# A graph network on one core: zero products left out of three gather loops, four waits put before GpSimd's gathers

## What is computed

```python
x = _layernorm(x + _L0_gnn_ref(x, L0_gnn_weights, src, edge_type_8, dst))  # per relation: mean of x[dst] over (src, type), times W[type]
x = _layernorm(x + _L1_gnn_ref(x, edge_index, ...))   # GCN: sum of dinv[src]*dinv[dst]*h[src] over dst, batch norm
x = _layernorm(x + _L2_gnn_ref(x, edge_index, ...))   # GATv2: 4 heads, scores of leaky_relu(xl[src]+xr[dst]), softmax over dst, feed forward
x = _layernorm(x + _L3_gnn_ref(x, edge_index, ...))   # two transformer convolutions: q[dst].k[src], softmax over dst, sum of attn*v[src]
```

## Time and profile before

| | us |
|---|---|
| median of 3 runs | 3878.28 (3877.59 to 3880.7) |
| the profiled execution | 3893.77 |
| its span, first to last instruction | 3892.1 |

### The profile page before, as it was taken

How to read it: one execution, slowest core, us unless ns; L and a number is a source line. 1 busy time by engine, 2 the same in 40 slices (tenths; PEclk the granted TensorE clock), 3 DMA queues, 4 the chain that set the end, 5 groups by cost and what they waited for, 6 DMA issues and landing times. The chain is left out here.

```text
span 3892.1 us, 57650 instructions
## 1 busy us (share of the span) xinstructions
PE 2947.8 (76%) x14303; PEld 2002.8 (51%) x14345; DVE 2492.3 (64%) x8135; ACT 1048.7 (27%) x2557; POOL 2423.7 (62%) x2427
## 2 busy tenths in 40 slices
PE   6987997746666567999977999766677776676773
PEld 3455895534444433444435777643465564364663
DVE  8886553251111377999988888873567775384876
ACT  3730664110000043333315666620011120010211
POOL 2747777647777347777754666117777734777770
PEclk8975557568888788999988999888798898888986
DMA  2222222322222147888851222026787755687872
GB/s 70 68 60 52 62 62 58 48 61 53 53 53 53 29 90 197 239 236 236 241 138 57 68 70 70 22 78 181 196 243 223 226 167 139 182 245 194 252 238 65
DMA packets 397387, 493.91 MB, mean 127 GB/s; under 512 B 64035, under 2 KB 293992, under 8 KB 397138
## 3 DMA queue, kind: packets, MB, share of 16 engines
q0 software_dynamic: 92160, 244.83, 24.3%
q1 hardware_dynamic: 304978, 245.98, 21.8%
HBM read 376.23 MB, written 114.36 MB: 126 GB/s over the span
## 5 line engine op out<-in xcount | busy, mean ns | idle before, releaser
L1918 POOL DMA_INDIRECT got<-kv_table,pair_src x832 | 839.3, 1009 | 495.4 <-issue 249.3
L686 POOL DMA_INDIRECT y_got<-y_table,y_idx x416 | 399.7, 961 | 166.2 <-issue 126.4
L1164 POOL DMA_INDIRECT got<-t_table,tile_src x392 | 378.3, 965 | 175.4 <-issue 118.8
L2167 PE MATMUL psum<-acc 125*128 x1664 | 285.1, 324 | 219.0 <-DVE h L1984 195.1
L1313 PE MATMUL sums<-msg,hot 128*125 128x260 f32 x1664 | 394.0, 390 | 31.3 <-POOL msg L1255 28.6
L2167 PEld LDWEIGHTS psum<-acc 125*128 125x128 f32 x1664 | 243.7, 224 | 297.1 <-issue 295.8
L2179 PE MATMUL psum<-h,acc 128*128 128x128 f32 x1664 | 324.0, 329 | 68.1 <-ACT hot_b L2142 37.3
L1313 PEld LDWEIGHTS sums<-msg,hot 128*125 128x125 f32 x1664 | 305.9, 189 | 119.1 <-issue 72.3
L1984 DVE TENSOR_TENSOR h<-psum,got 128x512 f32<-128x512 f32 x208 | 143.4, 690 | 348.1 <-DMA got<-kv_table,pair_src 315.1
L1255 POOL TENSOR_TENSOR msg<-rows,msg 128x512 f32<-128x512 f32 x208 | 246.3, 1204 | 188.1 <-DVE msg L1281 148.7
L628 PE MATMUL psum<-zeros 128*128 128x512 bf16 (+1 forms) x946 | 340.6, 490 | 3.5 <-issue 2.4
(11 more groups left out here) (506 smaller groups left out, 5705.3 us busy)
## 6 DMA issues: line engine op xcount, KB each, us to landing
v_rows<-got SPq DMA_DIRECT2D x208, 256.0 KB, 3.4
small<-v_rows SPq DMA_DIRECT2D x208, 256.0 KB, 4.8
dst_row<-dst_rows SPq DMA_DIRECT2D x312, 128.0 KB, 4.8
rows<-x_rows SPq DMA_DIRECT2D x104, 256.0 KB
x_rows<-small SPq DMA_DIRECT2D x104, 128.0 KB, 3.6
x_rows<-got_w SPq DMA_DIRECT2D x104, 128.0 KB, 4.5
got<-kv_table,pair_src POOLq DMA_INDIRECT x832, 3.8
y_table<-y_stage SPq DMA_DIRECT2D x25, 448.0 KB
```

The source lines that it names most:

```text
L686: pool.indirect_dma_start(out=got[:, slot, j, :], out_offset=None, in_=y_table[:, :], in_offset=bass.IndirectOffsetOnAxis(ap=m.y_idx[:, co ...
L1164: pool.indirect_dma_start(out=got[:, col % ring, :], out_offset=None, in_=table[:, :], in_offset=bass.IndirectOffsetOnAxis(ap=m.tile_src[: ...
L1918: pool.indirect_dma_start(out=got[:, slot, j, :], out_offset=None, in_=kv_table[:, :], in_offset=bass.IndirectOffsetOnAxis(ap=m.pair_src[: ...
L2167: last = t.matmul(work[:, j * P:(j + 1) * P], hot_t[:, g % 2, j // 2, j % 2, :], m.acc[:, bass.ds(ws[j], 1), 0:D].rearrange("q o d -> q (o ...
```

## The change

It takes three of the four calls of the helper out: 4 zero products behind each of 38 groups of the relation loop, 6 behind each of 92 groups of the GCN loop, 6 in each of 60 groups of each transformer. And it puts one more wait before GpSimd's DMAs in four loops: in the scatters of the sort for TensorE's `placed`, in the first ring of the relation's gathers for `counted`, in the GAT's gathers for `z_done` (all four sums of group g - 4 are made before the gathers of group g), in the transformers' for `q_done` (the queries of group g - 7 are spread before the gathers of group g).

```diff
@@ sort_edges, gpsimd
             for t in range(BY_DMA):
+                if 6 * t // 5 > 8:
+                    pool.wait_ge(placed, 6 * t // 5 - 8)
                 pool.indirect_dma_start(out=code_table[:, :], ...
@@ relation_layer, gpsimd
                 if g >= SL:
                     pool.wait_ge(used, g - SL + 1)
+                elif g > 2:
+                    pool.wait_ge(counted, min(4 * g - 8, groups))
@@ relation_layer, tensor
                 last.then_inc(used, 1)
-                if g >= 2 * SL:
-                    keep_busy(t, psum[0:Q, 6 * 512:7 * 512], zeros, Q, 4)
@@ gcn_sums, tensor
                 last.then_inc(used, 1)
-                if g < tile_groups - ROOM:
-                    keep_busy(t, sums[0:Q, 6 * 512:7 * 512], zeros, Q, 6)
@@ gat_scores, gpsimd
                 if g >= slots:
                     pool.wait_ge(turned, g - slots + 1)
                     pool.wait_ge(scored, (g - slots) // 2 + 1)
+                    pool.wait_ge(z_done, 4 * (g - 3))
                     pool.wait_ge(aside[slot], 32 * (g // slots))
@@ conv_layer, gpsimd
                 slot = g % 8
+                if g >= 7:
+                    pool.wait_ge(q_done, g - 6)
                 if g >= 8:
@@ conv_layer, tensor
                     for s in sums_due(c, k):
                         add(c - 1, s)
-                    if not len(sums_due(c, k)):
-                        keep_busy(t, psum[:, 0:512], zeros, P, 6)
```

## The result

The change makes the kernel slower by half a per cent: 3900.22 us median of 5 (3893.84 to 3908.23), beside 3879.77 for the kernel before (3877.59 to 3880.7). The ratio is 1.0056, interval 1.0043 to 1.0069, which is 17 to 27 us. The forecast was 3885, range 3877 to 3893. By the prediction's own line of 0.2% this is "slower", its second likeliest direction (0.42), and the time lies outside the range.

The account below looks back on a forecast made before the run. GpSimd's issue of gathers, 1.25 us each, was taken to bound the loops. Relation tail -1.7, transformer tails +0.75 and GAT wait +8.1 made +7.15 us on the median 3878.3: 3885, range 3877 to 3893.

Parts of the forecast that it names:

- The zero products in the loops: Relation, GCN and transformer loops: removing the products lowers TensorE's clock, but idle time hides it; cost 0.
- (c): Rival, loops: the lower TensorE clock costs time where cover is thin, up to 232 us; chance 0.02.
- The tails: Ends of loops: relation gains 1.7 us, GCN 0, transformers lose 0.75; -3 to +3 kept for the clock's phase.
- The waits that should not bind: Sort, relation's first ring, transformers: the added waits pass without a gap; cost 0, bounds 0 to 1 us.
- The wait that does bind: GAT gathers: waiting for the sums of group g - 4 stops GpSimd; +8.1 us, bounds 3.5 to 13.5.
- The release: GAT: a gather starts 0.74 us after the end of TensorE's sum, a figure taken from VectorE's releases.
- the prediction's replay: GAT, 98 groups recomputed by four rules from one trace's landings: 19 stops sum to 9.6 us, net +8.1.
- (b): Rival, GAT: the wait sets the loop's pitch, by later landings or slow TensorE groups; +13 to +18, 3891 to 3896; chance 0.18.
- The base: Whole kernel: the sum is added to the median 3878.3; the profiled execution's 15.5 us above it don't matter.
- (a): Rival, GAT: the wait passes after all, by faster release or earlier landings; +3 or less, 3877 to 3880; chance 0.22.
- (e): Rival, all four loops: the added waits never hold; counted as the same case as (a), without its own chance.
- (d): Rival, transformers: gathers themselves get shorter, saving over a third of 49 us, 18 us; total 3867; chance 0.08.

Follow-up runs that it names:

- second trace of before: The kernel before, unchanged, run again on a chip like the first: 3881.30 against 3881.09 us, ratio 1.0002.
- the tight wait alone: The kernel before with only the GAT wait on z_done (sums of group g - 4) added, on a chip like the first: 3900.18 us, ratio 1.0041.
- no_zero_b: The kernel before with all zero products of the three loops removed and no wait added, on a chip like the first: 3884.79 us, ratio 1.0007.

## Why the prediction was wrong

**What bounds the kernel** was read rightly, on the first chip: GpSimd's issue at 1.25 us a gather sets the four loops, and only the GAT wait reached it.

**The zero products in the loops: right.** Cost 0 forecast. The GCN, first gather to last sum, takes 509.9 us in after and 510.1 in before, with the clock at 0.50 instead of 0.81. Busy time of after from 870 to 970 us, and of before (us, then PE, PEld, DVE, ACT, POOL, clock, DMA share, GB/s):

```profile
870.00:970.00 100.00, 41.44 (x163) 35.59 (x162) 13.50 (x20) 0.00 (x0) 75.57 (x81) 0.50 0.20 53
```

```profile
870.00:970.00 100.00, 64.90 (x280) 42.76 (x279) 13.06 (x20) 0.00 (x0) 75.59 (x80) 0.81 0.21 53
```

GpSimd's busy time is the same to 0.02 us. In the first chunk of a transformer (2625 to 2775 us here) VectorE's product waits 2.5 us for TensorE over 30 groups, the 2.5 of the earlier trace rows, though the clock fell:

```profile
L1987 DVE TENSOR_TENSOR h<-psum,got 128x512 f32<-128x512 f32 x30 | 20.7, 691 | 94.3 <-DMA got<-kv_table,pair_src 91.8 <-PE psum L2170 2.5
```

So the clock fell from a mean of 0.829 to 0.737, and the time didn't follow: the rival (c), up to 232 us, did not come. The Trainium skill ("TensorE: Matmul & The Clock Gate", Part 1) advises against idle gaps. The clock fell with more idle time, as it says; the time would have followed only where something waits for TensorE.

**The tails: inside the +/- 3 that was kept, with both terms off.** Six traces on such chips have the zero products and four have not. From the first gather to the end of the closing products the relation takes 538.8 us in the mean with them, 537.1 without: -1.65, where -1.7 stood. That this fits so well is luck. The part that the zero products can touch, from the end of the last product to the end of the closing ones, is 3.86 us with them and 2.87 without, -1.0; the rest lies ahead of it, where nothing was taken from the path. TensorE at the relation's end, in after and in the second trace of before:

```profile
767.69 2.07 PE L967 MATMUL psum<-y_got,hot_w 128*125 128x128 f32 x8 [4.35 <-DMA y_got<-y_table,y_idx]
769.55 3.19 PE L976 MATMUL psum<-zeros 128*125 128x512 bf16 x7
```

```profile
767.83 2.07 PE L963 MATMUL psum<-y_got,hot_w 128*125 128x128 f32 x8 [2.99 <-DMA y_got<-y_table,y_idx]
769.69 1.74 PE L628 MATMUL psum<-zeros 128*125 128x512 bf16 x4
771.26 1.67 PE L974 MATMUL psum<-zeros 128*125 128x512 bf16 x7
```

The four zero products took 1.57 us there (granted clock 0.54), but the closing products behind them ran at 1.00 and took 1.67 us, where those of after ran at 0.50 and took 3.19, so the tail gains nothing against this trace; against the trace, where they took 2.80, it gains 1.3. That was the matter of phase for which +/- 3 was kept. In the transformers the tails (last gather to last sum) are 0.8 and 1.15 us longer without the zero products, 1.9 where 0.75 stood. So the tails give about +1 us, or +0.3 with the whole of the relation's difference, where -0.95 stood.

**The waits that should not bind: right**: ratio 1.0000, and no gap but the ordinary one.

**The wait that does bind: the mechanism right, the term mis-sized.** +8.1 was forecast, 3.5 to 13.5 as bounds; its own loop shows +15 to +16. Two parts of the working failed, and a third, its one trace, was thinner than it looked.

1. *The release.* 0.74 us was taken from VectorE's release. Group 31 of after, the last sum on TensorE and the gather that it lets go:

```profile
1628.32 0.81 PE L1651 MATMUL z<-xr,hot_t 125*128 x3
...
1629.97 0.94 POOL L1534 DMA_INDIRECT small<-x_table,pair_src  x1 [0.44 <-issue]
```

1629.97 - (1628.32 + 0.81) = 0.84. It is 0.84 or 0.85 in 22 of the 23 stops. The bounds had only an earlier release. With 0.84 the prediction's replay, which is an estimate, gives 1.7 to 2.2 us more, whichever trace's landings are used.

2. *One trace's landings.* The replay with the old 0.74 on the landings of six traces (the first two and the four of the second chip) gives 8.1, 13.5, 7.1, 7.0, 10.7 and 12.3, mean 9.8. The four traces of the third chip aren't in that; by the same rules, with landings read anew, they give 6.2 to 10.0, and all ten have a mean of 8.6. The mean landing is 9.02 us in the trace of the prediction and 9.01 to 9.12 in the other nine. So 8.1 was a fair mean for the rule behind it. What one trace couldn't show is the spread from execution to execution, and with a mean slack of 0.05 us it is wide: the prediction had seen that 0.3 us moved the answer to 13.5, and then gave rival (b) 0.18.

3. *The lead, which the prediction didn't have at all.* Once in 96 gathers, behind the first gather of groups 28, 52, 76 and 100, something keeps GpSimd's queue longer. Group 28, first in before, then in after:

```profile
1616.73 0.95 POOL L1533 DMA_INDIRECT small<-x_table,pair_src  x1 [0.30 <-issue]
1617.98 0.95 POOL L1533 DMA_INDIRECT small<-x_table,pair_src  x1 [0.30 <-issue]
```

```profile
1613.31 0.94 POOL L1534 DMA_INDIRECT small<-x_table,pair_src  x1 [0.30 <-PE z L1651]
1616.08 0.94 POOL L1534 DMA_INDIRECT small<-x_table,pair_src  x1 [1.83 <-issue]
```

The stops are 1.83, 1.86, 1.37 and 1.62 us, with leads before the group's first gather of 0.73, 0.70, 1.19 and 0.93 us: each pair sums to 2.56. The kernel with the tight wait alone has 0.70 and 1.86, 0.91 and 1.65, and once more 0.70 and 1.86, all 2.56 again, and 1.64 with 0.93. In the second trace of before one lead fell to 1.99 and the stop there is 0.57. Two kernels have one pair each that sums to 2.86 instead, 1.88 with 0.98 and 1.75 with 1.11; both are in group 52. Where the lead is 2.3 us or more the gap is the ordinary 0.30, as in all four places of the first trace of before. This is 5.5 us in after, 4.0 to 5.5 in the replays. The prediction took a passed wait to cost nothing, from gaps in front of groups whose waits are passed early; it didn't ask how early. This is the largest part of what was missing.

With the release and the lead put in, the replay gives 12.6 to 20.8 on the six traces, mean 16.4 (12 to 19 on all ten with the landings read anew, mean 14.1), and the loops measured 15.3 and 15.9.

**The base.** The sum was put on the median, since what the profiled execution had above it seemed not to matter. That was right: its 14 us were spread over many places and none lay in the GAT's gathers. Of the 14.8 us between 3885.4 and 3900.22, the GAT's loop has 7 to 8 and the tails one or two; the median of before rose by 1.5 with two more runs. The 4 us that are left no stage shows; they are less than the 10 us of the measured interval.

**The rivals.** (b) came nearest: slower by more, through the same wait. But neither of its two conditions is what came: the landings were not 0.3 us later, and the stops did not let TensorE's clock fall (its mean over the GAT's gathers is 0.98 in before and in after, with one slow group of 6.01 us in each). It was priced at 3891 to 3896, without the lead and with the short release. (a) and (e) are out on this chip: 27 gaps over 0.34 us, where (a) asked for fewer than five. (d) did not come: the 832 gathers of the transformers took 836.7 us for 839.3.

**The stated signs.** 104 zero products, PEclk 5 in the GCN, the gaps in front of L1534 (23 for the 19 forecast), and no wait of VectorE that grew by tens of us all came. The 1.70 us between the relation's last sum and its closing products are gone, with the closing products slow behind it. What (b) was to show, over 25 gaps in front of groups, did not come: the missing time is inside groups.

## What to carry to other kernels

An engine that runs at its own limit cannot win back a stop: here 11.7 us of stops in front of groups and 5.5 inside them made the loop 15.3 us longer. So a wait in its queue is priced by how its slack is spread over all turns, and not by the mean. Here the mean slack was nothing, and 23 of 98 turns stopped. Take the spread from several executions (the replay gave 6 to 13.5 us, by which execution's landings it used), or place the wait later among the instructions of the turn, where the same order cost nothing. A wait that is passed just in time also takes the queue its lead, and uncovers what the lead was hiding. And before work that keeps TensorE busy for its clock's sake is kept or taken out, look for a wait on TensorE: here 1424 such products bought 0.16% at the most (no_zero_b), and VectorE's products in the transformers waited 30.5 us for TensorE with them and 32.5 without.

## What the runs showed of the hardware

**A periodic step in GpSimd's queue.** It stands behind the same gathers, 113, 209, 305 and 401 of the GAT, 96 apart, wherever it shows in a trace, also in the slow chip's run of the unchanged kernel, where the leads are 0.70 and the stops 1.86, 2.16, 1.86 and 1.86. The added wait puts one more recorded instruction into each group, 24 more in each period, and moves the step by none. It goes with the gathers of this loop, then, and not with the number of recorded instructions. Its size does change with the code in one place: in group 52 lead and gap sum to 2.85 or 2.86 in all five traces without the added wait where the step shows, with and without zero products and on both kinds of chip, and to 2.56 in the three with the tight wait. The other loops of the slow chip's runs have no stops inside groups with this period. The Trainium skill ("Runtime: NRT & Kernel Launch", Instruction fetch mechanics) says that an engine's code comes in blocks of 256 instructions and that crossing a block is mostly hidden; a step at such a border should have moved with 24 more instructions in each period, so no run shows this one to be that. What it is stays open.

**A release from TensorE reached a GpSimd gather 0.84 us after the sum's recorded end**, one from VectorE 0.74 to 0.75 after its end (the earlier trace rows and the six other stops of that kind in four traces). TensorE's ends are modelled in the profile, which may be the whole of the difference.

**One chip is slower by more than any change here.** It took 4923 us for what others do in 3880 to 3885, with a granted clock of 0.747 for 0.829; there the change without its GAT wait gained 4.9%, and the GAT wait alone, which costs 16 us elsewhere, gained 34. That the wait's sign turns because GpSimd is held by others there is a reading and not shown. The whole change was not run on that chip.
